# Group-norm attention on one core: setup reordered, block sums moved to VectorE, bias products to ScalarE, and the low parts of the next image moved behind those of the probabilities

## What is computed

```python
xn = group_norm(x, gamma, beta)            # mean/var over H, W and the 16 channels of a group
xf = xn.reshape(B, N, C)
q = xf @ wq + bq
k = xf @ wk + bk
v = xf @ wv + bv
scores = jnp.einsum('bnc,bmc->bnm', q, k) * C ** (-0.5)
attn = jax.nn.softmax(scores, axis=-1)
out = jnp.einsum('bnm,bmc->bnc', attn, v) @ wp + bp
return out.reshape(B, H, W, C) + residual  # residual = x
```

## Time and profile before

| | |
|---|---|
| median of 3 runs (lowest to highest) | 2137.26 us (2137.19 to 2137.89) |
| the profiled execution: its own time | 2139.97 us |
| its span | 2138.3 us |
| granted TensorE clock, mean of the span | 0.997 of full |
| PE / VectorE / GpSimd / ScalarE busy | 98% / 84% / 41% / 35% |

### The profile page before, as it was taken

The page is one execution under the profiler, slowest core; times in us unless marked ns, Lnnn a source line. Parts: engine busy times, 40 slices in busy tenths (PEclk is TensorE's granted clock), DMA queues, the critical chain, the costliest instruction groups (busy, mean ns, idle before and its releaser), DMA issues.

```text
span 2138.3 us, 28427 instructions
## 1 busy us (share of the span) xinstructions
PE 2099.0 (98%) x9253; PEld 1730.9 (81%) x9253; DVE 1798.7 (84%) x2554; ACT 743.7 (35%) x1216; POOL 877.3 (41%) x475
## 2 busy tenths in 40 slices
PE   7999999999999999999999999999999999999999
PEld 5877888888888888888888788888878888888887
DVE  6898897988979888888888979889788898888865
ACT  4242332423333243332523324233332433335232
POOL 2452442524335244443524425243352434435253
PEclk9999999999999999999999999999999999999999
DMA  8003012030300203012030120303012030120101
GB/s 211 20 11 109 1 54 64 15 103 0 94 24 34 83 0 118 0 49 69 10 108 0 56 62 15 103 0 93 25 34 83 0 118 0 49 69 10 69 1 60
DMA packets 110268, 108.13 MB, mean 51 GB/s; under 512 B 8476, under 2 KB 74016, under 8 KB 110240
## 3 DMA queue, kind: packets, MB, share of 16 engines
q1 hardware_dynamic: 107984, 103.58, 16.0%
q10 hardware_dynamic: 2256, 4.20, 0.8%
HBM read 74.19 MB, written 33.55 MB: 50 GB/s over the span
## 4 chain that ended last, share of the span: by engine, by line
PE 51%; DVE 19%; issue 18%; POOL 7%; ACT 3%; DMA 0%; POOLq 0%; DVEq 0%; ACTq 0%
PE psum L1226 6%; PE psum L1228 6%; PE psum L1227 6%; PE psum L1251 5%; PE psum L1253 5%; PE psum L1252 5%; PE psum L1140 4%; PE psum L1139 4%; PE psum L1137 4%; DVE pt_lo L694 4%; POOL total_part L449 4%; DVE score L869 3%; DVE xn_lo L694 3%; POOL total_part L458 2%; PE psum L1057 2%
## 5 line engine op out<-in xcount | busy, mean ns | idle before, releaser
L1251 PE MATMUL psum<-v_hi,pt_hi 128*128 128x512 f32 x1024 | 401.4, 392 | 20.6 <-DVE pt_lo L694 17.4
L426 POOL TENSOR_TENSOR x_res<-x_res,out_bias 128x512 f32<-128x512 f32 x128 | 201.8, 1600 | 499.1 <-PE psum L1140 371.4
L1252 PE MATMUL psum<-v_lo,pt_hi 128*128 128x512 f32 x1024 | 399.2, 390 | 0.0
L1253 PE MATMUL psum<-v_hi,pt_lo 128*128 128x512 f32 x1024 | 399.0, 390 | 0.0
L694 DVE TENSOR_TENSOR pt_lo<-score,pt_hi 128x512 fp32r<-128x512 f32 x256 | 295.2, 1178 | 28.3 <-POOL total_part L449 25.0
L449 POOL TENSOR_TENSOR total_part<-total_part,score 128x512 f32<-128x512 f32 x192 | 309.1, 1610 | 16.6
L592 ACT ACTIVATE score<-psum 128x512 f32<-128x512 f32 x256 | 152.5, 596 | 342.3 <-PE psum L1228 341.9
L1251 PEld LDWEIGHTS psum<-v_hi,pt_hi 128*128 128x128 f32 x1024 | 192.6, 188 | 68.5 <-DVE pt_lo L694 25.1
L1253 PEld LDWEIGHTS psum<-v_hi,pt_lo 128*128 128x128 f32 x1024 | 192.6, 188 | 40.3
L1252 PEld LDWEIGHTS psum<-v_lo,pt_hi 128*128 128x128 f32 x1024 | 192.7, 188 | 39.1
L1226 PE MATMUL psum<-v_hi,xn_hi 128*128 128x512 f32 x512 | 201.7, 394 | 0.0
(11 more groups left out here) (162 smaller groups left out, 3992.2 us busy)
## 6 DMA issues: line engine op xcount, KB each, us to landing
x_res<-in_x_dram SPq DMA_DIRECT2D x128, 256.0 KB, 3.0
out_dram<-x_res SPq DMA_DIRECT2D x128, 256.0 KB, 2.2
x_blk<-in_x_dram SPq DMA_DIRECT2D x240, 128.0 KB, 3.2
score<-in_x_dram SPq DMA_DIRECT2D x16, 128.0 KB, 8.0
w_q<-in_L_conv_wq_dram SPq DMA_DIRECT2D x1, 1024.0 KB, 5.5
w_k<-in_L_conv_wk_dram SPq DMA_DIRECT2D x1, 1024.0 KB, 7.9
w_v<-in_L_conv_wv_dram ACTq DMA_DIRECT2D x1, 1024.0 KB, 9.1
w_p<-in_L_conv_wp_dram ACTq DMA_DIRECT2D x1, 1024.0 KB, 13.0
```

Of the source, the lines that this page charges most:

```text
L426: last = nc.gpsimd.tensor_tensor(at, at, out_bias[:, first:end], ALU.add)
L1251: nc.tensor.matmul(dst, hi[:, m, queries], v_hi[:, m, :], start=m == 0, stop=False)
L1252: nc.tensor.matmul(dst, hi[:, m, queries], v_lo[:, m, :], start=False, stop=False)
L1253: end = nc.tensor.matmul(dst, lo[:, m, queries], v_hi[:, m, :], start=False, stop=m == NT - 1)
```

## The change

It does the following.

1. SyncE waits until wp has landed before it issues the three wide vectors.
2. ScalarE makes the high parts of wv^T and of wp in turn instead of one after the other.
3. VectorE transposes quarter 3 of x ahead of the low parts of wv^T; the group variance is computed after two instead of four low parts of A's blocks; the four vector sums are taken after the first half of x is split and two chunks of `m_lo` are made.
4. The four block sums of A move from GpSimd to VectorE, behind the low parts of image 0's first-half queries; ScalarE makes their high parts among the queries of the second half, VectorE their low parts at the end of image 0's `xn_lo`; PE waits for them at the first product that uses one (S2) instead of ahead of image 1.
5. The products of w_p with bv are made in place by ScalarE (four activations); GpSimd adds the four chunks in three instead of six steps. The residual tiles 0 to 3 of image 0 move from GpSimd to VectorE (`first_residual`).
6. `first_bank(h, j)`: half 0 of image 0's queries starts in banks 0 and 1, which hold nothing that is waited for, and reaches the banks of M with j=2 and 3.
7. In every image but the last: all eight `pt_lo` of half 1 and the output tiles 1 to 3 come first on VectorE, then the four `xn_lo` of the next image.
8. `out_tile` 0 waits for the low part of v tile m only before step m (m from 2 on).

The diff, cut to its core, in the order of the file: constants, the load queue, GpSimd (from `block_sum` on), ScalarE (the four activations on `w_p`), VectorE (setup, first queries, the second half of an image), TensorE (first queries, output tiles):

```diff
-        BIAS_CHAIN = 2 * KC
-        BIAS_STEPS = 2 * KC + 1
+        BIAS_PARTS, BIAS_CHAIN, BIAS_STEPS = 3, 4, 5
...
-        def first_bank(j):
-            return work[(2 + j) % 4]
+        def first_bank(h, j):
+            return work[(2 * h + j) % 4]
...
+            sp.wait_ge(s_wload[3], 16)
             for vec, dst in ((bq, bq_wide), (bk, bk_wide), (bp, bp_wide)):
...
-            block_sum(S1, a21, a22, ALU.add)
-            block_sum(S3, a11, a21, ALU.subtract)
...
             root(0)
             pool.wait_ge(s_first, KC)
-            pool.wait_ge(s_bp, 1)
-            for k in range(KC):
...
-                nc.gpsimd.tensor_scalar(bias_part[:] if k else out_bias[:], w_p[:, k, :], bv_c[:, k:k + 1], None,
-                                        ALU.mult).then_inc(s_bias, 1)
...
+            pool.wait_ge(s_bp, 1 + KC)
+            nc.gpsimd.tensor_tensor(w_p[:, 0, :], w_p[:, 0, :], w_p[:, 1, :], ALU.add).then_inc(s_bias, 1)
+            nc.gpsimd.tensor_tensor(w_p[:, 2, :], w_p[:, 2, :], w_p[:, 3, :], ALU.add).then_inc(s_bias, 1)
+            pool.wait_ge(s_bias, 2)
+            nc.gpsimd.tensor_tensor(out_bias[:], w_p[:, 0, :], w_p[:, 2, :], ALU.add).then_inc(s_bias, 1)
+            pool.wait_ge(s_bias, BIAS_PARTS)
             nc.gpsimd.tensor_tensor(out_bias[:], out_bias[:], bp_wide[:], ALU.add).then_inc(s_bias, 1)
...
-                if starts(b):
-                    for i in range(TH):
-                        residual(b, i)
...
+            for k in range(KC):
+                nc.scalar.activation(w_p[:, k, :], w_p[:, k, :], ACT.Copy, scale=bv_c[:, k:k + 1]).then_inc(s_bp, 1)
...
             quarter_transpose(0, 2)
+            quarter_transpose(0, 3)
             setup_lo_parts(SET_WV, wv_t_hi, wv_t_lo)
-            quarter_transpose(0, 3)
...
-            setup_lo_parts(SET_M, m_hi, m_lo)
+            setup_lo_parts(SET_M, m_hi, m_lo, 0, 2)
+            dve.wait_ge(s_wide, 16 * 3)
+            dve.wait_ge(s_again[0], 16 * NI)
+            sum_products(0, KC)
+            setup_lo_parts(SET_M, m_hi, m_lo, 2, KC)
...
                 first_query_lo(0, 3)
+                block_sums_of_a()
...
                 for j in range(KC):
                     pt_lo_parts(b, 1, 2 * j, 2 * j + 2)
-                    if more:
-                        xn_lo_parts(b + 1, j, j + 1)
                     if j:
                         tile_out(b, j)
+                if more:
+                    xn_lo_parts(b + 1, 0, KC)
...
                     if h and j < 2:
-                        pe.wait_ge(s_tl, j + 1)
+                        pe.wait_ge(s_tl, j + 3)
                     elif h:
                         pe.wait_ge(s_free, j - 1)
+                    elif j == 2:
+                        pe.wait_ge(s_setr, lo_rank(SET_M) + 1)
+                    elif j == 3:
+                        pe.wait_ge(s_setr, lo_rank(SET_M) + 2)
                     elif j == 1:
-                        pe.wait_ge(s_setr, lo_rank(SET_M) + 2)
-                    elif j == 0:
-                        pe.wait_ge(s_setr, lo_rank(SET_M) + 1)
+                        pe.wait_ge(s_seth, SET_A_LAST + 1)
...
-                if i == 0:
-                    pe.wait_ge(s_free, n * SPLIT + PLACE[("v", 0, NT - 2)] + 1)
...
-                    if i == 0 and m == NT - 1:
-                        pe.wait_ge(s_free, (n + 1) * SPLIT)
+                    if i == 0 and m > 1:
+                        pe.wait_ge(s_free, n * SPLIT + PLACE[("v", 0, m)] + 1)
```

More of the change, by code:

```diff
@@ L113, in group_norm_attention @@
             w_k = sb("w_k", [P, KC, C], where=setup)
-        with ExitStack() as setup:
-            sb("above_bias_part", [P, NT + 3, C], where=setup)
-            bias_part = sb("bias_part", [P, C], where=setup)
         with ExitStack() as sums:
@@ L659, in image @@
                         first_query_hi(1, j)
+                        if j == 0:
+                            act.wait_ge(s_as, len(SUMS))
+                            for at in SUMS:
+                                nc.scalar.activation(ab_hi[:, at], ab_sum[:, at], ACT.Copy).then_inc(s_abh, 1)
                 else:
@@ L770, in v_lo_part @@
             def v_lo_part(n, m):
-                if starts(n) and m == 3:
-                    dve.wait_ge(s_bias, 2 * KC - 1)
                 dve.wait_ge(s_hi, n * SPLIT + m + 1)
@@ L901, in tile_out, with first_residual @@
                                                in1=at, op0=ALU.mult, op1=ALU.add).then_inc(s_y, 1)
+            def first_residual(i):
+                dve.wait_ge(s_bias, BIAS_STEPS)
+                dve.wait_ge(s_xr[i], 16)
+                at = x_res[:, i, :]
+                nc.vector.tensor_tensor(at, at, out_bias[:], ALU.add).then_inc(s_res, 1)
             def setup_lo_parts(u0, hi, lo, first=0, end=KC):
@@ L997, in image @@
                             token_stats(b + 1, *MEASURED[m])
+                    if starts(b) and m in (4, 5):
+                        first_residual(m - 4)
                 if more:
                     channel_stats(b + 1)
+                if starts(b):
+                    first_residual(2)
+                    first_residual(3)
                 tile_shift(b, 0)
@@ L1014, in image @@
                         norm(b + 1)
-                    if starts(b) and m == 4:
-                        for n, at in enumerate(SUMS):
-                            block_lo(at, len(WHOLE) + n + 1, ab_sum[:, at])
                 totals(b, 0)
@@ L1024, in image @@
                     pt_lo_parts(b, 1, 2 * j, 2 * j + 2)
-                    if more:
-                        xn_lo_parts(b + 1, j, j + 1)
                     if j:
                         tile_out(b, j)
+                if more:
+                    xn_lo_parts(b + 1, 0, KC)
+                if starts(b):
+                    for n, at in enumerate(SUMS):
+                        block_lo(at, len(WHOLE) + n + 1, ab_sum[:, at])
                 if more:
@@ L1104, in work_bank @@
                 elif what in (("v", 0, 0), ("v", 0, 1)) and starts(n):
[L1106 removed]
+                    pe.wait_ge(s_tl, 1 + what[2])
                 elif not (before and starts(n)):
@@ L1206, in first_queries @@
                         hi, lo = (part[:, k % 2, chunk(j % 2)] for part in block_parts(at))
-                        nc.tensor.matmul(first_bank(j), hi, xn_hi[:, k, tokens], start=k == 0, stop=False)
-                        nc.tensor.matmul(first_bank(j), hi, xn_lo[:, k, tokens], start=False, stop=False)
-                        last = nc.tensor.matmul(first_bank(j), lo, xn_hi[:, k, tokens], start=False, stop=k == KC - 1)
+                        nc.tensor.matmul(first_bank(h, j), hi, xn_hi[:, k, tokens], start=k == 0, stop=False)
+                        nc.tensor.matmul(first_bank(h, j), hi, xn_lo[:, k, tokens], start=False, stop=False)
+                        last = nc.tensor.matmul(first_bank(h, j), lo, xn_hi[:, k, tokens], start=False, stop=k == KC - 1)
                     last.then_inc(s_first, 1)
```

51 lines of the change are left out of this document (23 added, 28 removed).

## The result

| | before | changed |
|---|---|---|
| median (lowest to highest) | 2137.57 us (2137.19 to 2137.94, 4 runs) | 2112.23 us (2110.5 to 2113.47, 4 runs) |
| profiled execution: own time, span | 2139.97, 2138.3 us | 2110.5, 2108.8 us |
| granted clock, mean of the span | 0.997 | 0.999 |

The ratio is 0.9881, with a 95% interval from 0.9864 to 0.9898: faster by 1.2%, clear of the noise, as forecast. But 2112.2 us lies 10.2 us above the forecast of 2102 and 1.2 us above the upper end of the range.

What follows compares the result with a forecast made beforehand. PE, busy 98% of the span, was taken as the bound, so only its idle and slow time could be won: 12.0 - 2.9 + 7.3 + 19.7 - 0.7 = 35.4 us off 2139.97 gives 2104.6, median 2102 us; range 2097 to 2111.

Steps and rivals of the forecast that it cites:

- (b): Setup, PE's wait on `dev`: ready at 31.4, before PE asks at 31.9; 3.1 us won.
- (c): Setup, PE's wait on `m_lo` in M: no wait left, 4.4 us won, and 2.6 us of slow clock.
- Image 0: Image 0's output tiles: waits on v low parts and in tile 4 go, with slow clock; 7.3 us won.
- The loop's own term: Output tile 4, images 1 to 14: the `pt_lo` wait behind `xn_lo` goes; 19.7 us won.
- Rival 4: Loop: change 7 doesn't remove the `pt_lo` wait because GpSimd's totals set it; 2121 us; chance 0.05.
- term (a): Setup, `wp_lo` waits: wp's high parts start 1.5 us earlier; 1.3 us won of 2.1.
- rival 2: Setup: quarter 3 of x stays late, statistics come 2.3 us later, PE waits as much; 2104.3; chance 0.22 with rival 1.
- Setup, what comes: Start of `first_queries(1)`: GpSimd's adds alternate with `xn_lo`, query chunk late; PE waits 2.6, costing 2.9 us with restart.
- rival 1: Setup: GpSimd's adds block VectorE as one piece, clock falls; 5.2 instead of 2.9 us, 2104.3; chance 0.22 with rival 2.
- VectorE wins about 1 us itself ... I take nothing off in images 2 to 15: Loop: VectorE keeps ahead of the earlier PE, 1.5 us distance at v tile 0; only image 0's place gives back 0.7.
- That execution is 2.7 us above the median.: The earlier profiled execution's offset, carried over: forecast 2104.6 us becomes a median of 2102 us.
- rival 3: Loop: PE, 1.4 us earlier, meets VectorE at v tile 0 or queries; 9.8 us back, 2112 us; chance 0.16.

Runs made afterwards that it cites:

- loop_only: The kernel before with one edit, xn_lo of the next image behind all pt_lo: 2118.0 us, ratio 0.9909.
- adds_behind_v: The changed kernel with GpSimd's bias adds held until the low part of v tile 1 is made: 2107.3 us.
- wide_first: The changed kernel with the three wide vectors loaded right behind quarter 3 of x, without SyncE's wait for wp: 2110.5 us, ratio 0.9854.
- order_undone: The changed kernel with two setup moves undone (quarter 3's transposes behind wv_t's low parts, wv_t's high parts all before wp's): 2109.9 us.
- after_fit: The changed kernel with nine VectorE instructions fewer ahead of its loop, four low parts joined into one in three places: 2103.4 us, ratio 0.9843.
- best_fit: after_fit plus the edits of adds_behind_v and order_undone, with ab_lo between v tile 4's low part and image 1's norm: 2102.1 us, ratio 0.9835.
- ctl_repeat: The changed kernel again, unedited, as yardstick in group 1: 2111.1 us.
- ctl_2: The changed kernel, unchanged, as yardstick in group 3: 2109.9 us.
- ab_lo_early: The changed kernel with image 0's four ab_lo made in its score tiles 4 to 7: 2110.5 us.
- no_loop: The changed kernel with the loop edit undone, xn_lo again between the pairs of pt_lo: 2130.4 us, ratio 0.997.
- tail_only: The changed kernel with output tiles 5 to 7 getting bias and x from VectorE instead of GpSimd: 2222.5 us.
- combined: The changed kernel with the edits of adds_behind_v, order_undone and ab_lo_early at once: 2110.5 us.
- best_v_first: best_fit without its nine fewer instructions, and with the next image's low parts of v tiles 0 and 1 ahead of the last low sum of x: 2187.8 us.

## Why the prediction was wrong

**Right.** (b): the wait on `dev` went in full. (c): `m_lo` and its slow clock went. Image 0: 7.3 us forecast, 3.3 + 4.0 = 7.3 measured. The loop's own term: 19.7 forecast, 20.7 measured, and loop_only shows that the edit does it alone. Rival 4 (GpSimd's totals set that wait) is out. The new wait came where it was forecast, of 2.3 instead of 2.6 us, from the cause that was named (adds_behind_v), by alternation and not as one block of GpSimd.

**Wrong, four steps.** The forecast was 35.4 us off the span, and 29.5 came; and 4.4 more went in going from one execution to the median. The two largest are step 4 (4.4 us) and step 3 (3.8 us).

1. *Setup, term (a), and rival 2.* "1.3 us won" on `wp_lo` became 0.9 lost: the first `group_sum` starts at 31.10, not at 28.9, and in the kernel before it started at 30.22. I let quarter 3 land 2 us earlier because the wide vectors move behind it. It landed at 24.4 as before, and at 24.9 in wide_first, inside the spread of the others: the wide vectors, issued behind its pieces, had not held it up. So VectorE stood still for 3.73 us, and PE waited 1.1 on `wv_t_lo` and 0.7 on `mv`. Rival 2 was true, and at its price: `first_queries(0)` came 2.2 us late, and 2.3 was forecast for it. Undoing both moves brought 0.9 (order_undone).

2. *"Setup, what comes", with full clock behind the wait.* After 2.27 us of idle the clock fell to the lower level, 1.7 us, where I had taken from the earlier trace rows that 2.95 keeps it and 3.12 loses it. Two stops in one execution do not make a threshold: in loop_only 2.96 us of idle ahead of `dev` lost the clock, and five other traces kept it after the same 2.28 us as here (last section). What decides whether this 1.7 us comes is open. The wait and the clock cost 4.1 us, not 2.9 and not rival 1's 5.2; the slow clock of rival 1 came, but not its block of GpSimd.

3. *"VectorE wins about 1 us itself ... I take nothing off in images 2 to 15".* By the table, the loop's edit brings VectorE 0.65 us closer to PE's need (8.71 to 9.36), near the 0.4 that I had. The distance was about 1.1 us, not 1.5, because it ends at `u` and not at v tile 0. This alone gives back 1.3 us (loop_only), and 0.2 in after_fit. What I had no term for at all is the reload of code: another 1.0 us (9.36 to 10.37), which takes the changed kernel over the edge in all but one of 13 images, 3.2 us together. It was open to no reading of the earlier trace rows: in the kernel before there is no "issue" wait on VectorE and only 13 packets. Image 1 gave 1.3 back where I had 0.7.

4. *"That execution is 2.7 us above the median."* True of the one before; the changed kernel's profiled execution lay 1.7 us under its median. 2.7 + 1.7 = 4.4 us of the 10.2 are this step. An offset of one execution is chance and was not to be carried over; at the least it had to widen the range.

The first three together: 2.2 (late start of `first_queries(0)`) + 1.2 (wait and clock: 4.1 against 2.9) + 3.8 (4.5 given back, not 0.7) - 1.0 (loop) = 6.2, against 5.9 on the span; the parts are read to a few tenths. And 4.4. Without step 4 the median would have been about 2108, inside the range; it is the carried offset that took it 1.2 us past the end. The range was also put together too tightly: its high end of 2111 takes in rivals 1 and 2 together but only "most of rival 3", though the three don't exclude each other, and all of them came about in part. All three at their forecast prices make 2102 + 2.3 + 2.3 + 9.8 = 2116.4.

The trace agrees with the Trainium skill, page "SBUF — State Buffer", section "Who interferes with whom", as to who blocks whom, and after_fit fits with its being held for the whole instruction: one `xn_lo` of 2048 elements loses 1.0 us (3.32, against 2.28 in best_fit, where no add runs beside it), four of 512 lose 4.3 together (6.78 against 2.49). GpSimd's first two adds did not pass as one block: the first `xn_lo` ends at 52.84, and the second add, which starts at 52.25, takes 1.74 us, not 1.29. Of the reload, the Trainium skill, page "Runtime: NRT & Kernel Launch", section "Instruction fetch mechanics", says that a taken branch whose target is outside the window of code on the engine forces a load before the engine can go on. The 65 extra packets in 13 jumps and the stops that end 1.4 to 1.8 us behind a landing agree with that; which place in the stream makes the difference is not shown here.

## What to carry to other kernels

Look at the number of instruction packets and at "issue" waits of each engine before and after a change to a loop or to what stands ahead of it: code added ahead of the loop made every turn reload it here, at about 1 us of VectorE's time a turn, and two other orders of the body made that 3 to 7.5 us. Where two engines that block each other must run side by side, join the small instructions of the one that is waited for; it then waits once. Don't carry the offset of one profiled execution over to the median. And when rivals don't exclude each other, add their prices for the end of the range.

## What was not expected of the hardware

**The clock doesn't follow the length of a stop.** From one matmul's start to the next, a stop of 2.66 or 2.67 us at the same place of the program, the start of `first_queries(1)`, lost the clock in three profiled executions (the changed kernel, ctl_repeat, ctl_2) and kept it in five (order_undone, wide_first, ab_lo_early, no_loop, tail_only). The stop of 3.35 us ahead of `dev` in the setup kept it in the kernel before and lost it in loop_only, where PE's program is the same. One of 2.10 us lost it (combined). Ahead of all eight at the same place PE had been at full clock and without a longer pause for over 20 us; what decides is open.

**A turn of a loop can cost VectorE 7.5 us.** With the body ordered in another way (best_v_first) it stood 3.0 to 4.2 us ahead of `pt_hi` in each turn, and in most turns before that ahead of `u`; with a body of three instructions more (tail_only) it stood twice (3.2 and 4.3 us in one turn), at no semaphore. In the changed kernel's own body it was 0.2 to 1.4 us, and with nine instructions fewer ahead of the loop nothing.
